# Two-expert layer: adding each weighted result to the node's row in memory instead of storing two halves

## The reference, cut to what matters

```python
# x: 3125 x 256, normalised rows
topk_vals, topk_idx = top_k(x @ gate_w + gate_b, 2)
topk_w = softmax(topk_vals)
h = relu(x @ w1[e] + b1[e]);  expert_out[e] = h @ w2[e] + b2[e]
moe = sum over the 2 picks of topk_w * expert_out[pick]
y = x + moe
out = (y - mean(y)) / sqrt(var(y) + eps) * gamma + beta
```

## Time and profile before

| | us |
|---|---|
| median of 3 runs (1993.48, 1999.44, 2000.63) | 1999.44 |
| span of the profiled execution, first to last instruction | 2413.3 |
| expert stage, from its first fetch to the next stage's first load | 914.1 to 1166.2 |
| table stage | 1166.2 to 1245.7 |

### The profile page before, as it was taken

One profiled execution on the slowest core, in us unless ns is written; L12 is line 12 of the kernel. 1 busy time (PEld: TensorE's weight loads), 2 busy tenths in 40 slices (PEclk: granted clock), 3 DMA queues, 4 the chain that ended last, 5 costly groups with the idle time before them and its releaser, 6 DMA issues. The chain is left out here.

```text
span 2413.3 us, 38460 instructions
## 1 busy us (share of the span) xinstructions
PE 1891.3 (78%) x9911; PEld 1517.9 (63%) x9911; DVE 1125.8 (47%) x2791; ACT 1021.4 (42%) x3052; POOL 1104.5 (46%) x1499
## 2 busy tenths in 40 slices
PE   1368787877799858999455877787778789899699
PEld 1245454554466657999335766676767679777588
DVE  3532222222242374544664666565656669431322
ACT  2513343343353532333264555454545557454222
POOL 5547667666700004555375665565655550000243
PEclk7679999889999858999777888887888889999799
DMA  5636556565734026666544554555554553255553
GB/s 150 202 90 198 190 187 198 185 193 187 210 140 138 11 64 201 212 212 215 135 149 147 150 159 140 151 155 145 147 153 144 150 148 107 69 164 177 155 180 129
DMA packets 229197, 376.43 MB, mean 156 GB/s; under 512 B 66081, under 2 KB 114308, under 8 KB 228998
## 3 DMA queue, kind: packets, MB, share of 16 engines
q1 hardware_dynamic: 174820, 222.13, 31.0%
q0 software_dynamic: 52224, 150.15, 20.2%
q10 hardware_dynamic: 1954, 1.79, 0.2%
HBM read 275.38 MB, written 99.57 MB: 155 GB/s over the span
## 5 line engine op out<-in xcount | busy, mean ns | idle before, releaser
L1940 POOL DMA_INDIRECT msg_got<-y_dram,block_src x416 | 412.4, 991 | 293.5 <-DVE msg_prod L2012 139.7
L439 POOL DMA_INDIRECT ffn_w<-xn_dram,block_src x384 | 364.6, 949 | 219.2 <-issue 81.7
L1961 ACT ACTIVATE msg_scaled<-msg_plain,msg_w 128x125 f32<-128x125 f32 x1044 | 314.0, 386 | 280.1 <-DVE msg_plain L1993 234.6
L554 PE MATMUL sum_ps_bank<-ffn_w,sum_onehot 128*125 x928 | 270.5, 419 | 115.6 <-DVE sum_onehot L893 84.3
L554 PEld LDWEIGHTS sum_ps_bank<-ffn_w,sum_onehot 128*125 128x125 f32 x928 | 184.0, 206 | 264.6 <-issue 246.6
L881 DVE TENSOR_TENSOR agg<-sum_ps_bank,agg 125x256 f32 x232 | 98.4, 424 | 432.4 <-PE sum_ps_bank L554 216.5
L541 PE MATMUL sum_ps_bank<-sum_fc,sum_space 128*128 128x512 f32 x416 | 231.9, 644 | 68.9 <-ACT sum_space L639 48.3
L650 ACT ACTIVATE sum_space<-sum_ps_bank,sum_rec 128x128 f32<-128x128 f32 x416 | 131.0, 369 | 330.4 <-PE sum_ps_bank L541 159.5
L1982 PE MATMUL msg_ps_z<-msg_prod,msg_scaled 128*125 128x128 f32 x1416 | 207.5, 293 | 53.7 <-issue 53.0
L1982 PEld LDWEIGHTS msg_ps_z<-msg_prod,msg_scaled 128*125 128x125 f32 x1416 | 198.6, 206 | 72.4 <-issue 64.1
L2022 DVE TENSOR_TENSOR agg<-msg_ps_z,agg 125x512 f32 x232 | 159.4, 687 | 23.9 <-issue 5.2
(11 more groups left out here) (343 smaller groups left out, 3397.9 us busy)
## 6 DMA issues: line engine op xcount, KB each, us to landing
edge_w<-sum_space SPq DMA_DIRECT2D x52, 1040.0 KB
msg_w<-edge_w SPq DMA_DIRECT2D x174, 260.0 KB
ffn_run_w<-in_L_ffn_w SPq DMA_DIRECT2D x64, 512.0 KB
x_sb<-edge_w SPq DMA_DIRECT2D x58, 260.0 KB
ffn_rows<-agg SPq DMA_DIRECT2D x25, 448.0 KB
ffn_w<-in_L_ffn_w SPq DMA_DIRECT2D x16, 512.0 KB, 8.7
wd<-in_L_ffn_Wd SPq DMA_DIRECT2D x8, 1024.0 KB, 8.6
msg_got<-y_dram,block_src POOLq DMA_INDIRECT x416
```

Of the source, the lines that this page charges most:

```text
L439: pool.indirect_dma_start(got[:, (b + 1) % RING, u, :], None, k.x if b < RAW else k.xn_dram, bass.IndirectOffsetOnAxis(ap=k.block_src[:, b ...
L554: last = pe.matmul(ps_sum[n % ZB][0:P, :], onehot[n % OB][:, u, :], got[:, ds(need % RING, 1), u, :].rearrange("p o d -> p (o d)"), start= ...
L1940: pool.indirect_dma_start(got[:, (b + 1) % RING, u, :, :].rearrange("p k v -> p (k v)"), None, k.y_dram, bass.IndirectOffsetOnAxis(ap=k.bl ...
L1961: last = act.activation(scaled[s % MB][:, x, c, :], plain[s % MB][:, c, :], ACT.Copy, scale=w[s % RS][:, c, D + x:D + x + 1])
```

## The change

`m.results` now holds one row a node and 128 spare rows. `gin_and_route` writes `xn` there beforehand, from SP, after each group's rows (two more transfers a group), and fills the spare rows with a unit matrix by two small transfers. In `run_experts` DVE no longer makes `half`: `res` is the expert's output times its weight. POOL's send is an accumulating scatter: it adds the row to what stands in memory. Since both picks of a node may stand in neighbouring blocks, send(n) first waits until send(n-1) has landed. `combine_table` loads one row a node and does not add.

```diff
@@ gin_and_route, SP
+            for q in range(2):
+                sp.dma_start(m.results[N:N + TOK, q * 128:q * 128 + 128], k.ident[:, :]).then_inc(stored, 16)
             for i in range(NG):
                 sp.wait_ge(xn_made, G * (i + 1))
...
+                for a, b in SPANS:
+                    sp.dma_start(m.results[i * W:i * W + W, :].rearrange("(j p) d -> p j d", p=P)[a:b, :, :], k.xn_sb[a:b, i * G:i * G + G, :])\
+                      .then_inc(stored, 16)
-            sp.wait_ge(stored, 32 * NG)
+            sp.wait_ge(stored, 64 * NG + 32)
@@ Experts
-            self.results = nc.dram_tensor(f"{name}_results", [picks * N + self.blocks * TOK, D], F32, kind="Internal").ap()
+            self.results = nc.dram_tensor(f"{name}_results", [N + TOK, D], F32, kind="Internal").ap()
@@ pick_slots, DVE
-            if m.picks == 2:
-                chain(dve.scalar_tensor_tensor(node_f[:, :], m.pick1[:, :], float(N), node_f[:, :], ALU.mult, ALU.add))
@@ run_experts, DVE
-                    dve.wait_ge(half_made, n + 1)
                     dve.wait_ge(weight_step, 2 * n + 2)
-                    dve.scalar_tensor_tensor(res[s][:, :], res[s][:, :], weight[:, b, 1:2], half[b][:, :], ALU.mult, ALU.add).then_inc(res_made, 1)
+                    dve.tensor_scalar(res[s][:, :], res[s][:, :], weight[:, b, 1:2], None, ALU.mult).then_inc(res_made, 1)
...
-                dve.tensor_scalar(half[b][:, :], r[:, 0:D], 0.5, None, ALU.mult).then_inc(half_made, 1)
@@ run_experts, POOL
             def send(n):
                 pool.wait_ge(res_made, n + 1)
-                pool.indirect_dma_start(place_in, bass.IndirectOffsetOnAxis(ap=m.place[:, n:n + 1].bitcast(U32), axis=0),
-                                        res[n % S][:, :], None, bounds_check=last_row, oob_is_err=not m.last).then_inc(stored[n % S], 16)
+                if n >= 1:
+                    pool.wait_ge(stored[(n - 1) % S], 16 * ((n - 1) // S + 1))
+                pool.indirect_dma_start(m.results, bass.IndirectOffsetOnAxis(ap=m.place[:, n:n + 1].bitcast(U32), axis=0),
+                                        res[n % S][:, :], None, oob_is_err=True, compute_op=ALU.add).then_inc(stored[n % S], 16)
@@ combine_table, SP and DVE
-                for q in range(2):
-                    for a, b in SPANS:
-                        sp.dma_start(got[i][a:b, q, :, :], m.results[i * W + q * N:i * W + q * N + W, :].rearrange("(j p) d -> p j d", p=P)[a:b, :, :])\
-                          .then_inc(got_in[i], 16)
+                for a, b in SPANS:
+                    sp.dma_start(got[i][a:b, 0, :, :], m.results[i * W:i * W + W, :].rearrange("(j p) d -> p j d", p=P)[a:b, :, :])\
+                      .then_inc(got_in[i], 16)
...
-                dve.wait_ge(got_in[i], 64)
-                z = got[i][0:P, 0, :, :]
-                dve.tensor_tensor(z, z, got[i][0:P, 1, :, :], ALU.add).then_inc(z_made, 1)
-                dve.wait_ge(z_made, i + 1)
+                dve.wait_ge(got_in[i], 32)
```

## The result

The changed kernel takes 2102.05 us (median of 4 runs, 2091.85 to 2108.69), against 1997.2 us for the kernel before beside it. The ratio is 1.0523, with a 95% interval of 1.05 to 1.0547: slower by 105 us, where 43 were forecast.

A forecast was written before the change was run, and what follows sets the result against it. PE was taken to bound the expert stage before, POOL's wait after the change. Terms +54.8 - 0.2 - 7.9 gave +46.7 us, carried over to the timed kernel as 2042 us, range 1988 to 2110.

The forecast's parts named there:

- What bounds the kernel: Expert stage: PE sets the pace, busy 241.83 of 252.10 us, while POOL stands idle 1.41 us in one step.
- The new wait on POOL: Expert stage: each send waits for the previous landing, taken as 3.54 us against 2.69 of slack; 63 steps cost 53.6 us.
- the sentence on the issue: Expert stage: POOL's send issue stays at 1.04 us; each 0.1 us more would be 6.3 us.
- the 2.69 us of slack: Expert stage: time from a send's issue end to the next send's start; a landing within it costs nothing.
- The last landing: End of the expert stage: it waits for the last send's landing, 3.54 instead of 2.34 us, 1.2 more.
- First stage: First stage: SP's ten more stores and two small ones cost nothing, ending with some 11 us to spare.
- Table stage: Table stage: half the bytes loaded and five additions gone, -7.9 us in sum (bounds -3 and -12.8).
- The other three additions: Table stage: removed additions beside the chain of ACT and PE, given no more than that chain's gap, -1.9 us.
- Hidden: Rival, expert stage: the store lands within 2.69 us of its issue's end, PE stays the bound, 1991 us; chance 0.28.
- Read, then write: Rival, expert stage: read and write latencies add up to 5.60 us, total 2178 or 2147 us; chance 0.14.
- PE loses its clock: Rival, expert stage: gaps drop PE to 1.2 GHz and it is the bound again, 2226 us; chance 0.03.
- What would show it: Profile signs: POOL's idle ended by a transfer, step 4.58 us, PE some 80% busy, table stage's end 8 us nearer its start.

The follow-up runs named there:

- second trace of before: The kernel before, unchanged, profiled a second time: trace span 1996.4 us, median 1995.78 us, ratio 1.0001.
- first trace of before: The first profile of the unchanged kernel before, which the prediction read: span 2413.3 us, 414 us more than its timed runs.
- after: The profiled run of the changed kernel: median 2102.05 us, ratio 1.0523 to the kernel before.
- two tables: Changed kernel with even and odd blocks accumulating into separate tables, each send waiting for the send before the last: 2002.36 us, ratio 1.0041.

## Why the prediction was right in kind and wrong in size

**What bounds the kernel: right.** PE set the pace before, and POOL's slack in a step was what the change had to fit into.

**The new wait on POOL: right mechanism, mis-sized term.** The term was 63 x (3.54 - 2.69), from a step of 1.04 + 3.54 = 4.58. The step that failed is this term, given as 53.6 us, and in it above all the sentence on the issue: "1.04 us, I leave as it is". The issue is 1.59, and by the prediction's own price of 6.3 us per 0.1 that is 34.6 us. The landing is 3.76 in place of 3.54, another 13.9. The step before was 3.70 on average and not the 3.73 of one pair, another 2.1. So 53.6 + 34.6 + 13.9 + 2.1 = 104.2, and measured is 63 x (5.346 - 3.697) = 103.9. The issue had no bound from above in the sum; a longer issue counts in full because it stands in the same chain as the landing, while the 2.69 us of slack were computed with the short one.

The 3.54 came close for a reason that I had only half. It was taken from a fetch beside weight loads, as the row with the nearest neighbours. The runs show that an accumulating send lands in 2.98 without any, of which some 0.75 is POOL's time to go on, and that 0.8 us come from having both the fetch and the weights beside it.

**The last landing.** Forecast +1.2; from the last send to the next stage's first load it is 4.55 us (1101.13 to 1105.68) against 3.30 in the second trace of before (992.48 to 995.78): +1.25. The first send also comes 2.0 us later in the stage (764.31 - 747.10 against 759.58 - 744.41), which was not foreseen.

**First stage: right.** SP's wait for its last store is 3.5 us where it was 3.2 and is over before the stage's end; the granted clock and DVE's work there are those of before.

**Table stage: two terms right, one wrong.** The first load is 2.7 us sooner than in the first trace of before and 2.8 than in the second (forecast 3.0). To the first shift the stage gains 5.8 to 5.9 in all (forecast 6.0). The other three additions were given -1.9 and brought nothing: from the first group to the fifth ACT takes 47.4 us in after, 47.5 in the second trace of before and 45.3 in the first. Sum -5.0 for -7.9. What else holds these groups to 47 us I did not test.

**The rivals.** *Hidden*: refuted, since a landing of 2.98 in quiet is above 2.69 and the longer issue leaves only 2.14. Its trace evidence, quiet plain stores of 2.06 and 2.34, was right for a plain store (2.19 measured). *Read, then write*, 5.60: refuted; the add costs 0.79 us of quiet landing over a plain store (2.98 against 2.19), not a second full trip. *PE loses its clock*: refuted, 0.94.

For a plain scatter the Trainium skill's "DMA: Bandwidth & Descriptors", section "Anatomy of one DMA — SWDGE (gpsimd) path", agrees: an estimate of 2.3 us by its fit, beside 2.4 measured from the start of a quiet send's issue to its landing, and 2.19 from the issue's end to POOL's next start. For the accumulating one, "Collectives: The Full Stack", section "The bandwidth ceiling: the fold count and why AG ≠ RS ≠ AR", gave an estimate of 2.6 by a doubled byte term; measured by the same two counts are 3.7 and 2.98 in quiet, and 3.76 by the second among its neighbours. The measurement decides, and the issue, for which neither page gave a price, was the larger surprise.

**What would show it.** Of the signs named, POOL's idle time ended by a transfer, PE's busy share near 80% (76%), the first DVE operation 5.3 us after the load (5.6) and the unmoved first stage came as said; the step did not (5.35 for 4.58), the table stage's end came 5.0 us nearer to its start and not 8, and the last condition named for a wrong forecast, an issue longer by half a microsecond, is what happened.

## What to carry to other kernels

When a wait closes a chain on one queue, count every link anew, the issue of the changed instruction too: here the issue (+0.55 us) and the landing (3.76 us) add up 63 times, while the same instructions cost 0.23% of the time where nobody waits for the latest one. Give such a wait one more step of distance, as with two tables, before giving up the idea; and take the price of a landing from a row that has the same neighbours, since the neighbours were worth 0.75 us a step.

## What the runs showed of the hardware that I had not expected

- An accumulating indirect send of 128 rows of 1 KB holds POOL for 1.59 us, a plain one for 0.97 to 1.04; with 64 rows it is still 1.44.
- The software queue's packets doubled, 6144 to 12288, for the same bytes: an accumulating send of 128 rows makes 144 packets, a plain one 48.
- Fetches and weight loads beside the sends lengthen a step little by themselves (+0.17 and +0.20 us) and by 0.75 together.
- Where the wait for a landing stands as the last one in front of the next send, POOL goes on 0.80 us after the landing on average; where it stands right behind its send, 0.26 us. The cause is open.
